# A fused transformer block: score preparation, gate jobs and an expert count are moved between engines and places

## The reference

```
x = x + 0.5 * ffn(layernorm(x), ...)     # 8 experts, the top 2 of each token
x = x + attn(layernorm(x), ...)          # causal, 16 heads of 16
x = x + 0.5 * ffn(layernorm(x), ...)

# in ffn: N = 8192 tokens
cap = int(1.25 * N / E)                  # 1280
probs = softmax(x @ gate_w.T); top2_w, top2_idx = top_k(probs, 2)
counts = bincount(top2_idx, length=E)
keep = counts <= cap                     # an expert that drew more than cap tokens adds nothing
```

## Time and profile before

| what | us |
|---|---|
| median of 3 runs | 1411.99 (1410.11 to 1412.99) |
| the profiled execution's own time | 1411.99 |
| its span in the trace | 1410.3 |
| PE busy | 1277.3 (91% of the span) |
| DVE busy | 1093.3 (78%) |
| ACT busy | 941.6 (67%) |
| POOL busy | 399.7 (28%) |
| the prologue, to the first `st` of batch 0 | 101.9 |

### The profile page before, as it was taken

One profiled execution on the slowest core, in us unless ns is written; L12 is line 12 of the kernel. 1 busy time (PEld: TensorE's weight loads), 2 busy tenths in 40 slices (PEclk: granted clock), 3 DMA queues, 4 the chain that ended last, 5 costly groups with the idle time before them and its releaser, 6 DMA issues.

```text
span 1410.3 us, 24418 instructions
## 1 busy us (share of the span) xinstructions
PE 1277.3 (91%) x8356; PEld 549.6 (39%) x8356; DVE 1093.3 (78%) x3527; ACT 941.6 (67%) x1697; POOL 399.7 (28%) x508
## 2 busy tenths in 40 slices
PE   4679999999999999999999999999999999999883
PEld 2223333443344433444344433444334443434332
DVE  3579888878878788878878788888888788779643
ACT  2227777677768677676777677677776777676661
POOL 2312422232323323233213323232222323222120
PEclk8759999999999999999999999999999999999997
DMA  3771334144335424254333434354431343330000
GB/s 116 123 125 29 68 58 77 25 87 98 68 57 96 77 63 72 36 98 98 57 69 58 84 66 72 64 98 86 68 69 31 56 91 69 57 68 31 1 16 18
DMA packets 56344, 95.17 MB, mean 67 GB/s; under 512 B 8208, under 2 KB 49808, under 8 KB 50064
## 3 DMA queue, kind: packets, MB, share of 16 engines
q1 hardware_dynamic: 54176, 92.30, 34.9%
q10 hardware_dynamic: 2032, 1.19, 0.3%
HBM read 59.91 MB, written 33.55 MB: 66 GB/s over the span
## 4 chain that ended last, share of the span: by engine, by line
PE 60%; DVE 17%; ACT 13%; issue 5%; POOL 2%; DVEq 2%; DMA 0%; POOLq 0%; ACTq 0%
PE o_bank L1190 14%; PE s L1171 13%; PE st L1158 11%; PE misc L1109 8%; ACT q_stack L773 5%; DVE s L930 5%; ACT probs L786 5%; PE misc L1104 4%; PE misc L1135 4%; DVE max_full L934 3%; PE misc L489 3%; POOL probs L660 1%; DVE o_tok L1020 1%; ACT qk L746 1%; DVE stats L456 1%
## 5 line engine op out<-in xcount | busy, mean ns | idle before, releaser
L786 ACT ACTIVATE probs<-st 128x512 f32<-128x512 f32 (+1 forms) x1216 | 633.2, 583 | 199.2 <-PE st L1158 108.7
L930 DVE CUSTOM_DVE_ANT_0 s<-s,causal 128x128 f32<-128x128 f32 (+3 forms) x1024 | 494.6, 502 | 136.8 <-PE s L1171 134.0
L1171 PE MATMUL s<-k_stack,q_stack 96*128 96x512 bf16 (+3 forms) x1536 | 496.7, 336 | 32.2 <-DVE max_diag L930 14.3
L1158 PE MATMUL st<-q_stack,k_stack 108*128 108x512 bf16 (+3 forms) x1536 | 486.7, 330 | 23.9 <-ACT probs L786 21.6
L934 DVE TENSOR_REDUCE max_full<-s 128x1 f32<-128x512 f32 x512 | 350.0, 684 | 34.5 <-PE s L1171 32.9
L1190 PE MATMUL o_bank<-probs,v_aug 128*17 128x512 f32 (+3 forms) x3072 | 324.1, 494 | 8.9 <-POOL probs L660 6.6
L660 POOL TENSOR_SCALAR_AFFINE_SELECT probs<-probs 128x512 f32<-128x512 f32 x256 | 163.7, 644 | 545.6 <-ACT probs L786 545.2
L1171 PEld LDWEIGHTS s<-k_stack,q_stack 96*128 96x128 bf16 x1536 | 149.6, 98 | 391.1 <-DVE max_diag L930 186.1
L1158 PEld LDWEIGHTS st<-q_stack,k_stack 108*128 108x128 bf16 x1536 | 149.5, 98 | 145.9 <-ACT probs L786 54.0
L672 POOL TENSOR_TENSOR qk<-qk,parts 128x512 f32<-128x512 f32 x64 | 76.3, 1193 | 320.9 <-ACT parts L746 320.9
L773 ACT ACTIVATE q_stack<-misc 12x2048 bf16<-12x2048 f32 x64 | 119.7, 1871 | 43.5 <-PE misc L1141 42.2
(11 more groups left out here) (88 smaller groups left out, 840.1 us busy)
## 6 DMA issues: line engine op xcount, KB each, us to landing
part_dram<-parts SPq DMA_DIRECT2D x128, 192.0 KB, 2.8
k_stack<-part_dram SPq DMA_DIRECT2D x192, 128.0 KB, 7.0
q_stack<-part_dram SPq DMA_DIRECT2D x32, 384.0 KB, 5.0
x_all<-x SPq DMA_DIRECT2D x16, 512.0 KB, 10.5
q_stack<-part_dram SPq DMA_DIRECT2D x32, 256.0 KB, 7.3
out<-x_all SPq DMA_DIRECT2D x7, 1024.0 KB, 10.9
q_stack<-part_dram SPq DMA_DIRECT2D x32, 128.0 KB, 8.8
w_qk<-wqk_t ACTq DMA_DIRECT2D x1, 512.0 KB, 5.3
```

The source lines that it names most:

```text
L786: nc.scalar.activation(probs[:, g % 2, h - part:h + 1, 0:width], st_bank[i % 3][:, 0:share * width] .rearrange("p (h c) -> p h c", c=width ...
L930: nc.vector.tensor_tensor_reduce(out=bank, in0=bank, in1=causal[:, CW - width:CW], scale=1.0, scalar=-BIG, op0=ALU.add, op1=ALU.max, accum ...
L1158: score = nc.tensor.matmul(st_bank[i % 3][:, part * width:(part + 1) * width], k_stack[0:KROWS + MROWS, hg, h, jb * P:(jb + 1) * P], q_sta ...
L1171: nc.tensor.matmul(s_bank[u % 3][:, 0:width], q_stack[0:KROWS, hm, h, ib * P:(ib + 1) * P], k_stack[0:KROWS, hm, h, j0:j0 + width], start= ...
```

## The change

It has four parts.
1. **Prologue order.** The `qk` halves of group 1 leave their places between the `v` jobs and join the others in the loop, so that six halves stand at positions 2, 11, 20, 29, 38 and 47.
2. **`ones`.** The four copies go from VectorE to ScalarE, in the same place of the list, as ACTIVATE Copy.
3. **`lg0` and `lt0`.** In group 2 they go from positions 12 and 17, and in group 3 from 12 and 28, to 7 and 12 in both.
4. **The total.** The matmul with ones is replaced by `partition_all_reduce` on GpSimd into a tile of its own, `total`. In the last batch GpSimd does it at position 2 of group 2, and VectorE decides at position 10, where it was 7. `misc` is no longer used for it.

```diff
-    "end": (24, 26, 29, 32, 35), "top2": 17, "before": ((12, 17), (12, 28)), "xload": 0, "top0": (2, 4), "count0": 2,
-    "total0": 7,
+    "end": (24, 26, 29, 32, 35), "top2": 17, "before": (7, 12), "xload": 0, "top0": (2, 4), "count0": 2,
+    "decide0": 10,
...
-    plan += [(3, "use", "v", j) for j in range(2)] + project(1, 0) + [(3, "use", "v", j) for j in range(2, 4)]
-    plan += project(1, 1) + [(3, "ones", hq) for hq in range(NG)]
+    plan += [(3, "use", "v", j) for j in range(4)] + [(3, "ones", hq) for hq in range(NG)]
...
-    halves = [(hq, c) for hq in range(2, NG) for c in range(2)]
+    halves = [(hq, c) for hq in range(1, NG) for c in range(2)]
...
+            def all_counts(layer):
+                eng.wait_ge(counted, layer + 1)
+                nc.gpsimd.partition_all_reduce(total[:, :], counts[:, :], P, ADD_REDUCE).then_inc(totalled, 1)
...
+                elif kind == "count0":
+                    all_counts(0)
...
             run(eng, attention, moe_pool, idle, lambda: None)
+            all_counts(1)
             if_kept(eng, 1, lambda: moe_pool(1))
...
+                elif kind == "ones":
+                    if sig.spec:
+                        hq = a[0]
+                        eng.wait_ge(max_rows_ready, MPARTS)
+                        rows = nc.scalar.activation(k_stack[KROWS:P, hq, :, :],
+                                                    row_of_head[:, :, :].to_broadcast([32, HG, S]), ACT.Copy)
...
-            def decide(layer, taken):
+            def decide(layer):
 
                 vec = nc.vector
-                vec.tensor_scalar(kept[:, 0, :], misc[:, 0:E], float(CAP), None, ALU.is_le).then_inc(taken, 1)
+                eng.wait_ge(totalled, layer + 1)
+                vec.tensor_scalar(kept[:, 0, :], total[:, :], float(CAP), None, ALU.is_le)
...
-            eng.wait_ge(counted, 2)
-            total_counts().then_inc(totalled, 1)
             if_kept(eng, 1, lambda: moe_tensor(1))
```

More of the change, by code:

```diff
@@ L26 @@
 AX = mybir.AxisListType
+ADD_REDUCE = bass.bass_isa.ReduceOp.add
 B, S, D = 8, 1024, 256
@@ L180, in step_plan @@
     if hg >= 2 and nxt and spec:
-        for u, what in zip(PLACE["before"][hg - 2], ("lg0", "lt0")):
-            put(u, ("use", what, hg - 2))
+        put(PLACE["before"][0], ("use", "lg0", hg - 2))
+        put(PLACE["before"][1], ("use", "lt0", hg - 2))
     if hg == 1 and spec:
@@ L190, in step_plan @@
             put(PLACE["count0"], ("count0",))
-            put(PLACE["total0"], ("use", "total0"))
+            put(PLACE["decide0"], ("decide0",))
     if hg == NG - 1 and not nxt:
@@ L376, in program @@
         late_counts = sb("late_counts", [P, E])
+        total = sb("total", [P, E])
         kept = sb("kept", [P, 1, E])
@@ L424, in program @@
         totalled = sem("totalled")
-        total_taken = sem("total_taken")
         flag_ready = sem("flag_ready")
@@ L729, in evict @@
             def evict(sig, b, n, hg, what, *a):
-                if what in ("otr", "wo", "total0"):
+                if what in ("otr", "wo"):
                     return
@@ L809, in handle @@
                     eng.wait_ge(bias_scaled, 1)
+                elif kind == "ones":
[4 more added lines that the diff above has]
+                                                    row_of_head[:, :, :].to_broadcast([32, HG, S]), ACT.Copy)
+                        if hq == NG - 1:
+                            rows.then_inc(max_rows_ready, 1)
             def idle():
@@ L987, in handle @@
                                                 ALU.mult).then_inc(bias_scaled, 1)
[L988 to L994, removed]
-                            rows.then_inc(max_rows_ready, 1)
                 elif kind == "top0":
@@ L1002, in handle @@
                     count_chosen(tables[1][0])
-                elif kind == "use" and a[0] == "total0":
-                    eng.wait_ge(sig.misc_full, n("use", 1))
-                    decide(0, sig.misc_free)
+                elif kind == "decide0":
+                    decide(0)
                 elif kind == "top2":
@@ L1053, in _ @@
             nc.vector.tensor_tensor(counts[:, :], counts[:, :], late_counts[:, :], ALU.add).then_inc(counted, 1)
-            eng.wait_ge(totalled, 1)
-            decide(1, total_taken)
+            decide(1)
             if_kept(eng, 1, lambda: moe_vector(1))
@@ L1087, in moe_tensor @@
                 moe_experts(eng, layer, None, chunk, expert)
-            def total_counts():
-                return nc.tensor.matmul(misc[:, 0:E], v_aug[:, 0, 0, HD:VW].to_broadcast([P, P]), counts[:, :],
-                                        start=True, stop=True)
             v_taken = {}
@@ L1117, in fill @@
                     last = tensor_gate_logits(misc, x_t[:, :, a[0] * CW:(a[0] + 1) * CW])
-                elif what == "total0":
-                    eng.wait_ge(counted, 1)
-                    last = total_counts()
                 elif what in ("lt", "lt0"):
```

## The result

The changed kernel takes **1428.15 us** (median of 4 runs, 1427.39 to 1428.34) against 1411.38 for the kernel before in 4 runs between them (1410.11 to 1412.99). The ratio is 1.0117, 95% interval 1.01 to 1.0135, so it is 16.8 us slower; 1423.6 was forecast, with a range of 1416 to 1433. The profiled execution took 1428.08 us, its span is 1426.2.

What follows compares the result with a forecast made beforehand. The kernel was taken as bound by the order in which work passes between engines, TensorE carrying most. Prologue 5.8, `lg0`/`lt0` 2.8, last batch 3.0 and end 0 sum to 11.6 us on 1411.99: 1423.6, range 1416 to 1433.

Steps and rivals of the forecast that it cites:

- the likeliest case: Whole kernel: slower, 1423.6 us, from a longer prologue, gate jobs and last-batch reloads, nothing at the end; chance 45%.
- prologue, parts 1 and 2: Prologue: later position 3, two more fills and two casts in VectorE's loop make it 5.8 us longer.
- reload at the start: GpSimd's library reload before its first `rstd`: hidden in a 0.24 us gap, so 0 us.
- rival 1: Start: the reload becomes real, 6.9 us less 4.1 us idle, adding 2.8 us, total 1426.4; chance 25%.
- `lg0` and `lt0`: Groups 2 and 3, 14 places: TensorE waits 1.1 us for `misc` at position 7; net +0.2 us each, +2.8 us.
- last batch: GpSimd, last batch: two reloads of 6.9 us around the reduction delay masks and `rstd`, +3.0 us.
- end: Between last count and decision: reload covered by idle time, reduction (0.6 us) stands for the matmul (0.59), 0 us.
- Start of the loop: Prologue: ScalarE's `ones` take 14.3 us; first scores 0.9 us sooner, but position 3 reaches VectorE 2.0 us later.
- Two more fills: Prologue loop: fill at 38 costs 2.0 us (bounds 0.3 and 2.4), at 47 1.0 us, two casts 0.8 us.
- rival 4: Groups 2 and 3: not slower; shorter logits ahead of `mtr` give 0.6 us a place, 1406 to 1412; chance 8%.
- Rival 2: GpSimd: code loads at the first call, not at the reload; last batch +8.7, end +6.9, total 1436; chance 8%.
- Rival 3: GpSimd: reloads cost nothing to speak of; only prologue and gate jobs remain, 8.6 us, total 1420.6; chance 14%.

Runs made afterwards that it cites:

- parts 1 and 2: Kernel before with only the group 1 `qk` halves moved into the prologue loop and the four `ones` copies on ScalarE: 1409.77 us, ratio 0.9994.
- Part 2 alone: Kernel before with only the `ones` copies moved to ScalarE, the group 1 halves where they were: 1416.32 us, ratio 1.0044.
- the reduction at the end alone: Kernel before with only the second layer's total on GpSimd, the first layer's still the matmul: 1419.62 us, ratio 1.0059.
- the late start: Kernel before plus one GpSimd memset of the query stack (13.77 us) at the start, no library changed: 1419.83 us, ratio 1.0067.
- part 4 alone: Kernel before with only the total of both layers by `partition_all_reduce` on GpSimd: 1423.25 us, ratio 1.0091.
- the library set back: Both layers' totals on GpSimd as the only change to the kernel before, plus one GpSimd multiply at the end that reloads the other library: 1419.4 us.
- part 3 alone: Kernel before with only `lg0` and `lt0` moved to positions 7 and 12: 1418.38 us, ratio 1.0056.
- the two with `lg0` moved: Kernel before with `lg0` at 7, `lt0` left at 17 and 28: 1419.9 us; and with `lg0` at 8, `lt0` at 12: 1411.26 us.
- the one with `ones` spread: Kernel before with group 1 halves in the loop and the `ones` copies on ScalarE at loop positions 3, 12, 24 and 33: 1401.81 us, ratio 0.9929.
- part 1 alone: Kernel before with only the group 1 `qk` halves moved into the loop, `ones` still on VectorE: 1405.77 us, ratio 0.9966.

## Why the prediction was right, and where it was not

The time lay in the range and the likeliest case had the right sign and kind, but that is in part luck: wrong terms cancelled. The prologue was put 7.2 us too dear, and the start, the gate jobs and the last batch 8.3 + 4.4 + 0.8 = 13.5 us too cheap. Half of what was measured comes from the start, which the likeliest case put at nothing. What each term forecast, and what its experiment measured:

| term | forecast | measured |
|---|---|---|
| prologue, parts 1 and 2 | +5.8 (2 to 9) | -1.4 (1409.77 against 1411.14) |
| reload at the start | 0; +2.8 in rival 1 | +8.3 |
| `lg0` and `lt0` | +2.8 (-8 to +10) | +7.2 |
| last batch | +3.0 (0 to 11) | +3.8 |
| end | 0 | 0 |
| sum | 11.6 | 17.9; the whole change 16.8 |

**Start of the loop.** Right where it was worked out: the loop begins 65.62 - 40.26 = 25.4 us behind the second `v` fill, 1.2 us sooner than before (forecast 0.9), and position 3 comes 2.1 us later (forecast 2.0). The copies took 14.13 us together, 3.53 each (forecast 14.3).

**Two more fills.** Wrong. The step that failed is "the one at 38 is like that at 29, which cost VectorE 2.00 us", and with it that "the fills at 11, 20 and 29 stand where they stood": it took the clock of the old loop for the new one. The fill at 38 ran at the full clock (1.88 us) and cost 0.41 us; in the kernel where it took 3.15 us it cost 1.85, near the 2.00. The one at 11, at the old place, got 1.9 us cheaper. The low bound of 0.3 was there for just this, but only for the new fill, and I never asked it of the old ones. From position 3 to the first `st` the changed kernel takes 40.6 us and the kernel before 41.6: 1.0 gained, where +3.8 was forecast. Part 2 alone has four fills in the loop, as before, with 1.88 us at 11 like the changed kernel, and takes 38.7 us there. By these single traces the old fills gave 2.9 us back, and the two further ones with their casts cost 1.9, half of the 3.8. The clock alone moves this stretch: in the eight kernels whose loop is the old one it takes 39.8 to 41.6 us.

The -1.4 of the table is not the prologue's alone. In the trace of parts 1 and 2 the first `st` is 0.85 us early, and 1.0 us lies ahead of everything that changed: the `v` fills ran at full clock (1.99 us) and one at 3.78 before (at 28.46 us). Between batches 1 and 5 it gains 1.7 us more, and in group 3 of the last batch it loses 1.2, where its granted clock is 0.50 from 1335 to 1338 us and 1.00 in the kernel before. The 1.7 us come in three steps, at 400, 736 and 990 us of the kernel before, and the same steps are in every kernel with `ones` off VectorE and in none of the others. VectorE's list is four instructions shorter there. In the kernel before it stands idle for 0.44 us five times with nothing shown that ended it, for one:

```profile
733.48 0.50 DVE L945 CAST max_parts<-max_diag 128x16 bf16<-128x16 f32 x1 [0.44 <-issue]
```

Counted in VectorE's list these places have 964, 1524, 1863, 2197 and 3320 instructions ahead of them. In parts 1 and 2 and in part 2 alone three are left, behind 963, 1862 and 3319, and so ahead of other jobs. The steps at 400 and 736 us lie within 3 us behind one of the five, the one at 990 does not. That the steps come from these places is possible and not tested.

**The start.** This is rival 1, and it is shown: the library left by the execution before sets the gap. The main case put it at 0, rival 1 at 25% and with the wrong price, since it took the 6.9 us of a reload in mid-kernel; it is 12.9 us here. By its own working, less the 0.24 us that stood there before and the 4.1 us of slack of the earlier trace rows, the right length gives 12.9 - 0.2 - 4.1 = 8.6, and 8.3 were measured with the reduction at the end alone (8.7 with the late start, whose `rstd` is another 1.2 us later). Why the reload at the start takes longer than one in mid-kernel no run shows.

**`lg0`, `lt0`.** The mechanism was right: a wait of 1.1 us (0.93 measured) and a loss of 0.7 us for VectorE (0.68). The term that was mis-sized is what was taken off again, down to "+0.2 us a place", for the shorter job ahead of `mtr` and one fill fewer behind. By position 17 nothing has come off for it, and behind that 0.13 us, where 0.5 was taken: 0.42 us a place in the trace, and 7.2 / 14 = 0.5 between the medians. The sentence against rival 4, that VectorE has no idle time between the two places to make good what it loses, was true against my own discount as well. With 0.7 for it the term would have been 9.8, with the measured 0.5 it is 7.2.

**Last batch.** Reloads of 6.02 and 7.65 us (6.9 taken), a reduction of 0.43 us (0.6 taken), and 3.8 us in time (3.0). The working had +0.8 at the mask behind the first reload and +3.3 behind the second. The first cost nothing: no product waits for a mask before the second, in any of the three kernels with both reloads. The loss comes at the second: TensorE waits 3.17 us there for the mask behind `rstd`, 2.23 with part 4 alone and 2.41 with the library set back, and over group 2 the shift grows by 4.5, 1.6 and 3.0 us.

**The end.** Right: a reload covered by 14.88 us of idle time and a reduction that stands for the matmul.

**Rivals.** Rival 2, code that comes in at the first call, is refuted: at the end the reduction starts 0.13 us after the count is done, with no gap, though it is the first call since the reload, and in the last batch the 6.02 us begin when the masks end, 4.9 us before the count is ready. So that rule, "GPSIMD Engine Reference", section 2.1 of the Trainium skill, is about right here in the size (approximately 6 us, against 6.02 and 7.65 in mid-kernel, but 12.92 at the start) and right in that no instruction shows it, but not in where it falls: the load stands at the reload, ahead of the call, and can be hidden. Rival 3 is refuted by part 4 alone (+12.1), rival 4 by part 3 alone (+7.2).

What is still open: why the granted clock takes the level it does in the loop. Kernels whose TensorE list is the same up to 30 us show both levels from 20 to 35 us (below), so I can't call the 14 idle microseconds of TensorE ahead of the loop its cause. What it is worth can be read off: of the kernel before, part 3 alone and the two with `lg0` moved, whose prologues are the same, the first `st` comes at 101.89, 99.24, 98.72 and 101.52 us. A shift of up to 3 us at the first `st` of a single trace is thus no finding. The 1.1 us by which the parts add to more than the whole is within what single kernels vary by.

## What to carry to other kernels

A library routine on GpSimd is priced at its reloads, not at its work: count every change of library, the one into the next execution too, and see for each whether anything waits for GpSimd there. Of the four here two were hidden, and the two that something waited for cost 8.3 and 3.8 us. A job in a shared bank should be placed where the bank is already free; at position 7 it cost 7 us over 14 places, and at 8 nothing. Time that a move opens is only worth having where the engine next in line has work: `ones` was free on VectorE as soon as the cast ahead of it was gone, and dear on ScalarE in one piece.

## What the hardware showed that was not expected

- A reload of GpSimd's library left gaps of 6.0 to 7.7 us in the middle and at the end (6.02, 7.65, 7.56), but of 12.6 to 12.9 us at the start of an execution. Where the library was the one already loaded, the gap was 0.24 to 0.49 us.
- The program leaves a trace in the next execution: one multiply at the end, with the reload ahead of it, takes 12.1 us from a gap at the start (12.62 to 0.49). What another program leaves behind no run shows.
- ScalarE took 3.53 us for a copy of 32 x 4096 in bf16, VectorE 2.46 us.
- TensorE's granted clock in three stretches of 5 us, from 20 to 35 us, was 1.00 in each in the kernel with parts 1 and 2 and the one with `ones` spread, 0.73, 0.50 and 0.75 in the kernel before and in part 1 alone, and 0.81, 0.85 and 1.00 with part 3 alone, whose prologue is that of the kernel before. One profile each; the second `v` fill of these kernels starts at 31.0 to 32.9 us by it.
- VectorE stood idle for 0.44 us at five places of its list with nothing shown that ended it, and taking four instructions out of the list moved those places onto other jobs.
